# Three row normalisations of a decoder tile computed on GpSimd instead of VectorE, in tiles 0 to 13, with all engine lists written anew

## The reference, cut to what matters

```
x = layernorm(x + attn(layernorm(x)*g + b, memory))   # 8 heads, 256 memory slots, 3 retrieval steps, entmax-1.5
x = layernorm(x + xattn(x, ctx))                      # 16 heads, 64 context rows, softmax
x = layernorm(x + x @ (W * scale).T + bias)           # dense, 256 to 256
layernorm(y) = (y - mean(y)) / sqrt(var(y) + 1e-5)    # over the 256 values of a row
```

## Time and profile before

| | |
|---|---|
| median of 3 runs | 880.46 us (878.66 to 974.31) |
| the profiled execution, its own time | 881.4 us |
| its span, first to last instruction | 879.5 us |
| busy: PE, DVE, ACT, POOL | 817.2, 766.5, 736.5, 490.1 us |
| DMA | 17.63 MB, mean 20 GB/s |

### The profile page before, as it was taken

One profiled execution on the slowest core, in us unless ns is written; L12 is line 12 of the kernel. 1 busy time (PEld: TensorE's weight loads), 2 busy tenths in 40 slices (PEclk: granted clock), 3 DMA queues, 4 the chain that ended last, 5 costly groups with the idle time before them and its releaser, 6 DMA issues.

```text
span 879.5 us, 18277 instructions
## 1 busy us (share of the span) xinstructions
PE 817.2 (93%) x5598; PEld 699.7 (80%) x5598; DVE 766.5 (87%) x1915; ACT 736.5 (84%) x1781; POOL 490.1 (56%) x2304
## 2 busy tenths in 40 slices
PE   6999998899999989999988999999999998999964
PEld 5878887688898878988877888888878876887852
DVE  3699998999999999989998999999989999997451
ACT  3589997999998999979899899989989899987310
POOL 4144357465655664666754666674665757566232
PEclk9999999799999989999999999999999999999986
DMA  8900002000000000000000000000000000000000
GB/s 271 226 1 1 18 20 77 9 10 5 1 1 1 1 2 0 2 16 8 15 3 1 8 1 4 2 2 1 10 19 3 7 2 1 1 8 1 1 25 16
DMA packets 24215, 17.63 MB, mean 20 GB/s; under 512 B 11760, under 2 KB 23536, under 8 KB 23856
## 3 DMA queue, kind: packets, MB, share of 16 engines
q1 hardware_dynamic: 23872, 16.13, 6.6%
q0 software_dynamic: 240, 0.27, 0.2%
HBM read 14.30 MB, written 2.10 MB: 19 GB/s over the span
## 4 chain that ended last, share of the span: by engine, by line
PE 65%; DVE 16%; ACT 11%; POOL 4%; issue 2%; DMA 1%; SPq 0%; POOLq 0%
PE banks L1318 26%; PE banks L1341 10%; PE banks L1329 7%; PE banks L1406 6%; PE banks L1365 5%; DVE moments L859 5%; ACT work L769 4%; DVE top L839 3%; ACT work L760 2%; PE banks L1189 2%; PE banks L1376 2%; ACT work L781 2%; PE banks L1398 2%; PE banks L1419 1%; DVE work L879 1%
## 5 line engine op out<-in xcount | busy, mean ns | idle before, releaser
L859 DVE BATCH_NORM_STATS2 moments<-work 128x6 f32<-128x512 f32 x576 | 377.1, 687 | 9.4 <-ACT work L769 6.3
L1318 PE MATMUL banks<-weights_s,work 128*128 128x256 f32 x1536 | 356.4, 385 | 1.5 <-ACT work L760 0.7
L769 ACT ACTIVATE work<-work,neg_u 128x256 f32<-128x256 f32 x768 | 332.8, 524 | 22.6 <-DVE neg_u L871 17.3
L1318 PEld LDWEIGHTS banks<-weights_s,work 128*128 128x128 f32 x1536 | 288.4, 193 | 46.5 <-issue 7.7
L760 ACT ACTIVATE work<-banks,neg_low 128x256 f32<-128x256 f32 x384 | 154.5, 499 | 5.2 <-DVE neg_low L850 4.9
L839 DVE MAX8 top<-banks 128x8 f32<-128x256 f32 x384 | 141.2, 415 | 9.6 <-PE banks L1318 8.5
L1009 POOL TENSOR_TENSOR resid_sum<-moments 128x8 f32<-128x8 f32 x144 | 30.5, 212 | 210.4 <-DVE moments L859 209.1
L1329 PE MATMUL banks<-ident,work 128*128 128x128 f32 x768 | 113.1, 283 | 20.5 <-ACT work L752 8.1
L781 ACT ACTIVATE work<-banks 128x512 f32<-128x512 f32 x192 | 113.7, 613 | 15.8 <-PE banks L1329 15.6
L1329 PEld LDWEIGHTS banks<-ident,work 128*128 128x128 f32 x768 | 90.6, 145 | 37.5 <-issue 15.8
L1341 PE MATMUL banks<-weights_s,work 128*128 128x256 f32 x512 | 115.0, 380 | 0.0
(11 more groups left out here) (159 smaller groups left out, 1079.1 us busy)
## 6 DMA issues: line engine op xcount, KB each, us to landing
work<-in_L_xattn_Wo_dram SPq DMA_DIRECT2D x2, 1024.0 KB, 11.2
out_dram<-work SPq DMA_DIRECT2D x16, 128.0 KB, 1.8
work<-in_L_xattn_w_kc_q_dram SPq DMA_DIRECT2D x2, 768.0 KB, 5.8
rows<-in_L_xattn_Wq_dram SPq DMA_DIRECT2D x1, 1536.0 KB, 14.3
rows<-in_x_dram SPq DMA_DIRECT2D x1, 1536.0 KB, 6.6
work<-in_L_attn_Wq_dram SPq DMA_DIRECT2D x1, 1024.0 KB, 9.2
work<-in_L_attn_Wo_dram SPq DMA_DIRECT2D x1, 1024.0 KB, 12.1
work<-in_ctx_dram SPq DMA_DIRECT2D x32, 32.0 KB, 2.2
```

The source lines that it names most:

```text
L769: ins = nc.scalar.activation(q_resid[:, j, h, :], q_resid0[:, j, h, :], ACT.Relu, bias=small["neg_u"][:, j, h:h + 1])
L859: ins = nc.vector.bn_stats(moments[:, j, 2 * q:2 * q + 2, :].rearrange("p h k -> p (h k)"), r.rearrange("p h n -> p n h"))
L1318: ins = nc.tensor.matmul(ps_scores[:, h, :], lhsT, w[:, h, t, :], start=(t == 0), stop=(t == CT - 1))
```

## The change: what it does, and the diff

For tiles 0 to 13, `norm` is no longer a stage of DVE. Its instruction, with the same operands, follows the seventh instruction of `rstd` on POOL in the same stage, and signals `row_step` as before. That is 42 instructions (14 tiles with three each). In tiles 14 and 15 `norm` stays on DVE. The lists of turns of all five engines are new.

```diff
@@ tile_stages
-    dve, dve_tail = dve + after, dve_tail + after
+    dve_tail += after
+    dve = [what for what in dve if what[0] != "norm"] + once("residual", 1) + once("residual", 2)
@@ tile_turns (the last line of each string)
-        "PE": ...
-              "fffffbfbbcbcccccccbeebeeeceeccfefcfffffdfddcddddcdccdddeceedeeeceddeddfefeeffeffddfeefeefffefeffffff",
+        "PE": ...
+              "ffffffbbbcbcccccccebeebeececceeffcfffffdfddcdddcdccdddceedeeeeceddeddeefeffefffdfdeefeefffefeffffff",
-        "POOL": ...
-                "bdeeffcddbffdedeeecfceeffdfeecffcddbfefdedfedcefgffef",
+        "POOL": ...
+                "beedfcfbddffbdedeeecfceeffdfecefcfddeffddecfeefgeffdf",
-        "SP": "04216357109238ba4d7cfe6589dcbaef",
+        "SP": "20156374a20983176bed54fc8ab9dcef",
...
@@ POOL, stage rstd, behind the seventh instruction
+                        if in_tail(p, j):
+                            return
+                        pool.wait_ge(rstd_step[j], step(RSTD_OPS))
+                        if s == 2 and p:
+                            pool.wait_ge(out_stored[j], p * 16)
+                        nc.gpsimd.tensor_scalar((q_out if s == 2 else q_row)[:, j, :], q_y[:, j, :], row_mv[:, j, 0:1],
+                                                row_rstd[:, at], ALU.subtract, ALU.mult).then_inc(row_step[j], 1)
```

More of the change, by code:

```diff
@@ new lines, in tile_turns @@
+        "DVE": "hhhhhh0hhh0h00100h000021h00110011001h1020h1202102h20h0h21h102h02h02h11211h211h011110201h1002122h0020"
+               "202h020221h021212h11h0001h11010h210120312h1011h22h101222213h21213023033h1203h13331223h3103230323h023"
+               "20322h303323hh3hh23113111000403603012033300035303031030300337033010323212322131331223221121202341434"
+               "21441212114a418440141433232344344030434334134344595454425522202333345234325445450535434443354b535452"
+               "45445643636546465556656d65546116360476767677c6464166566754761566557755575766575474657657655715675674"
+               "555456475775464226564144466762464752675655546444764477646774465266477775547574e435537777565757656635"
+               "6534778725578888575773888f86886566885858448676387667776648864868569968696989684999977797986979796988"
+               "97988599899888596878a77aa5aa579479aa8aa888aa978aa89aa998a8a8858988aaaa797a798a979a769897688858988989"
+               "9789869bb6b8bb8889b98989bb9aabaa9ab896b8a8a8aba8b897abab79b89b99aaba9a999babb8a97ca9cbaacbbcca6cb9a7"
+               "ccac9a99ccbb9c9bcbcc79c9cb99bba9ab9c9ababcaccaabbabcbca988aab8bdaaacadddad7babbbdd8cbcdbbdcccaddaaac"
+               "cccda8cacdaddcbcdcdcbdcbcbdbddcbacbcbce9d9dcedcbceeeb9b98bebebbdedbedbdeed9bbbdbdcdbebbdaadedeeccddc"
+               "eddecaadbdeeececf9fcdefcdffddecaceffffccffefadfffbdfefedeecfcfffbdfecdfdcfdedeecccebcefbfefeffceecff"
+               "fefdecdddbfefeeefffefdedcefdddfdbfdfdffdedfedfefeedcceedeeddcefeffeffeceefffefedeefeefceeeffffdfdfdd"
+               "cfefeffdfffeeeeeedefefeeffffffegfffffefg",
@@ new lines, in tile_turns @@
+        "ACT": "hhhhhhhh01h0000h0000211101h00h0h22h2h2h0h1h01h11002h0111102h22110h1100h022h2210102h02h102h2111h02010"
+               "h1211h0h3222211112h202h03h3033020h33h3302222h333h310111021031022333131311000043363352000033332072003"
+               "0303321202211132233223011141040443131841411443031323442443232494445550343045010022242342344335255544"
+               "434553133536566264103546616456554155776666a73b741666655556167715751754544664675554576772215544454656"
+               "5625627744447675567252675642424477677366636746477475445557334265767336575635387777884874888347855555"
+               "6685646748787864476646488c988999856899996766556989989868775798889854daaa9ae95777569aa9aa858858aaaa88"
+               "788969698589a7aa7a77798898879966898898a6b9b9b6a78b8668f98aa99a97bab798b9b8aaa8a88b99b989bb7aa6a9abbb"
+               "bc79cc7bcb899aa7ac7c7cc9ab999bbabca9c9c9c9a9babab9b8a88c8aaaab7bccbcdbdcdacda9bab8bb8ca8c8ccdddbdaca"
+               "bacccaaddaddcbcc9cbb89b9dd9cdcdcaceebbedbb99de99bdbbebdddeacabcbbeebdbddbadaeecce9eacabdcdadadfefefe"
+               "fbcecabfefffcedcdfdfdeffeedebdffbcffcdcdcdfdefeeebbfffbfbcccecceefefcffeedebdeddffcffddedecfdcfffeee"
+               "efdfcdddedeecfeffdfcceecceefdfffdedceeeeddfedddfdffeffefffefedeeffefffff",
@@ new lines, in tile_turns @@
+        "POOL": "hh000010101022211112200022010111122200131332233232h3hhh000010033300332111323221011414422343433440120"
+                "2335550443435524455660630664164671757557575155466614747466224416654777455527755334227753888656683683"
+                "7646485869649977799898986754574aaa88aa885aa7979958588989766889b9bb688aaabb99a9ab98b76a6a7ccc99cc9b9b"
+                "bac7acbaab9a7a7bb88dddaccac8ddccbdacdcbb8b998bebee9bbdddecedadab9e9eccdcafffadffacffceeecbbdceeffddf"
+                "beedfcfbddffbdedeeecfceeffdfecefcfddeffddecfeefgeffdf",
```

7 lines of the change are left out of this document (added).

## The result

The changed kernel took 889.86 us (median of 4 runs, 889.23 to 890.60), beside 880.84 us for the kernel before. One of the four runs of before, 974.31 us, fell in a slower state of the chip and is left out of the ratio, which is 1.011, with a 95% interval of 1.0089 to 1.0131. The change is slower by 9.0 us on these medians, by 9.4 beside the 880.46 us that the other three runs of before have as their median. Its time lies 2.9 us above the top of my range. The forecast, a gain of 5 us, had the wrong sign. The execution that the profile shows took 890.03 us, with a span of 888.1 us; the one of before had 881.4 and 879.5.

What follows compares the result with a forecast made beforehand. PE was taken as the bound, DVE and ACT nearly level where PE stalls. Gains of 5 (relief) and 2 (sooner rows) less 2 (Newton steps) took 881.4 to 876.4, by the runs' median 875.5, called 875 us; range 863 to 887.

Steps and rivals of the forecast that it cites:

- relief and port: DVE's work: 18.7 us relieved less 2.7 us held at the memory port, of which a third, 5 us, was credited.
- sooner rows: Normed rows start a step after their roots on POOL; PE's one wait of 2.2 us credited as 2 us gained.
- Newton steps: Newton arithmetic queued behind the normed row on POOL comes later, at most 23 us summed; charged a tenth, 2 us.
- lists 0: New order of turns on all engines: not priced, bounded by PE's idle 22.5 us either way, taken as nothing.
- DVE loses 42 instructions: Normed rows leaving DVE: 42 by 0.404 us is 17.0 us, with 1.7 us idle before them 18.7 us.
- PE is the bound: Rival: PE busy for 96% of 190 to 800 us, so nothing moves, 878 to 884 us; chance 0.22.
- I take 0.55 us: Length of one normed row on POOL, between a fill's 0.34 us and the two-tensor biased row's 729 ns.
- That load is hidden by POOL's idle time: POOL's added 23 us (14 to 31) was held covered, since POOL waited 139 us on `moments` alone.
- The port, 2.7 us: DVE instructions held at the port shared with POOL: 42 x 0.23 x 0.28 us; bounds nothing and 23 us.
- third rival: Slower by the lock: POOL's normed row delays Newton arithmetic and holds DVE's clip or weights, 887 to 900 us; chance 0.16.
- The end from 840 keeps its length: Sign for the forecast: the last stretch, tile 15's serial chain, stays as long, as its normed row stays on DVE.
- ACT's wait for `neg_u`: Sign that the lock decides: this wait, with longer means of L874, L871 and L879, grows well over 13 us.

Runs made afterwards that it cites:

- e12_none_old: Kernel before with its old lists, 42 normed rows struck from DVE, a 0.19 us POOL instruction in each row's place, normalisation of tiles 0 to 13 left out: 879.51 us.
- e12_none_new: Changed kernel, new lists with mended end, a 0.19 us POOL instruction in place of each normed row, normalisation of tiles 0 to 13 left out: 883.60 us.
- e6_whole_end: Changed kernel with list ends mended: DVE's flag before the last normed row, POOL's third roots of tiles 14 and 13 and tile 13's row moved: 885.86 us.
- e4_old_lists: Changed kernel, rows on POOL, but with the lists of the kernel before, the moved rows only struck from DVE's: 895.41 us, ratio 1.0183.
- e13_both: Kernel before, rows kept on DVE, and the same 42 rows also made on POOL into a buffer nobody reads: 902.52 us, ratio 1.0239.

## Why the prediction was wrong

The sum that the runs give, by medians, from 880.84: relief of DVE, net of 0.19 us a row on POOL, -1.3 (e12_none_old); new lists' body +4.1 (e12_none_new against e12_none_old, 883.60 - 879.51); the rows on POOL in those lists +2.3 (e6_whole_end against e12_none_new); the end of the lists +4.0 (the change against e6_whole_end). By the ratios the four are -1.2, +4.0, +3.5 and +3.4. Each term is a step from one kernel to the next, so they must add up to the whole, and that they do is no check. The medians come from different chips, so each term has about 2 us of doubt.

Beside my own terms (relief and port -5, sooner rows -2, Newton steps +2, lists 0) this says where the 14 us between the forecast and the result lie: 8.1 in the lists that I took at nothing, 3.7 in the relief, 2 in the sooner rows, and almost none in the rows' cost on POOL (2.3 where I had charged 2). That last number is close by luck. The new lists had made the row cheap, at a price of their own; in the order that I knew, the same rows cost 17 us, and the whole change 16 instead of a gain of 5. With the rows on POOL the lists as a whole save 6.4 us (16.1 to 9.7 by the ratios), so neither half of the change stands alone.

Step by step, as I put them:

- **"DVE loses 42 instructions", 17 us off its work: right in kind, less in amount.** The groups' busy times fell by 14.4 us: 17.3 less in the rows, 2.9 more elsewhere, most of it in the held lines below. What reached the end was mis-sized. I took "a third, 5 us"; it was 1.3. I had read that PE carries 65% of the chain. But that kernel doesn't prove the rival "PE is the bound" either: 4.2 us more stood ready near the end and were lost behind `worst_all`, a stand of POOL that my sum doesn't have. Whether a third is wrong without it stays open.
- **"I take 0.55 us": failed.** 1.24 us measured, outside both bounds. I took the two-tensor instruction for the dearest form because it reads most. The nearest row by shape was not the nearest by form: no instruction on POOL of before was a two-operation one with values a partition, so the upper end had no row behind it.
- **"That load is hidden by POOL's idle time", charged with "a tenth, 2 us": failed; in the old order it is the step that turned the sign.** In the lists that I knew, the row costs 16 + 1.2 = 17 us beside the kernel with 0.19 us in its place, which is 0.4 us for each of the 44 us added. Even at about my 0.55 us it is not a tenth: at 0.40 it costs 2.3 us, at 0.61 6.7, so around 5 us where I charged 2. The wait of 139 us for `moments` is POOL idle while nothing is due; what counts is the moments in which it is not. The row of one tile runs then in front of another tile's Newton step. I named that very queue, and who waits for it, and then priced it by an average.
- **"The normed row comes sooner", +2 us: not seen.** No kernel has this part alone. In e12_none_old the readers may go as soon as the root is there, and that and all of DVE's relief together are 1.3 us net.
- **The port, 2.7 us: the holding is there, the price is not shown.** The means of the four DVE lines after (L872, L875, L880, L848) are 202, 228, 373 and 261 ns, where they were 169, 219, 367 and 255. That is (33 + 9 + 6) x 48 ns and 6 x 192 ns, 3.5 us. It looks like my 2.7, but the rows are not its cause in the main: in e12_none_new, which has the new lists and no row, the four lines are already 2.2 us above before, so the rows add 1.3. In the old lists they add nothing (+1.7 in e12_none_old, +1.5 in e4_old_lists, which lost 16 us). And my formula with the measured length gives 42 x 0.52 x 0.62 = 13 us, ten times what the rows add; the nearness of 2.7 to 3.5 is luck. Two of the lines, after:

```profile
L872 DVE SCALAR_TENSOR_TENSOR neg_u<-delta,neg_limit x48: 116/156/758, 38.1 to 796.5; 128x8 f32<-128x8 f32 x48
L875 DVE TENSOR_TENSOR neg_u<-neg_u_raw,neg_limit x48: 115/168/992, 46.0 to 808.9; 128x8 f32<-128x8 f32 x48
```

  The trace holds single instructions (116 ns at the shortest, 758 at the longest), so it agrees with the lock rule of the Trainium skill, "SBUF — State Buffer", section Who interferes with whom, in kind; the 3.5 us, and DVE's unchanged 766.7 us in e13_both, say that it is not what made the kernel slower. My third rival was right in its sign and its time, and had two causes, "the lock" and the Newton steps behind; only the second holds, and for the old lists. In the changed kernel most of the loss is the order's.
- **The rule of one-input work at line rate:** the Trainium skill, "GPSIMD Engine Reference", section Engine selection, sets GpSimd beside VectorE: about twice as slow for two-input work, roughly line-rate for one-input. By the rows, the product of two tensors on POOL takes 0.72 us, and DVE's two-tensor sum of the same shape (one of them from PSUM) 0.42, so 1.7 times as slow, which agrees in the main. The normed row, with one tensor, takes 1.23 us on POOL and 0.404 on DVE, three times as long, which doesn't agree. The measurement decides.
- **"The new lists ... take nothing": failed, and it is the largest part of the miss in the changed kernel.** They make the row cheap, 2.3 us (3.5 by the ratios) instead of 17, but for that the order of the whole body costs 4.1 us and the last tile 4.0. My bound of 22.5 us on either side holds the net of both; the middle of a bound is not a price. "The end from 840 keeps its length" was wrong for the same reason. I had the new lists before me in the diff, and the place of `g`, the flag, against the last `f` stands in the last line of DVE's.
- **"What would show it":** ACT's wait for `neg_u` was to tell the slower rival, "well over 13 us". From 190 to 800 it is 13.9 after, so by that sign it would have been denied. The lists had made that wait short again, and the time went into PE's other waits; e4_old_lists, with 28.5 beside 17.3 over the span, shows it as the sign predicted.

What stays open: why the new lists' body costs 4 us by itself, and which engine's list does it; no kernel here has one engine's old list with the others' new ones. Open too is what the relief of DVE brings without POOL's stand behind `worst_all`.

## What to carry to other kernels

An engine with 44% of idle time is not a place where work is free. Ask what stands behind the new instruction in that engine's queue and how long the chain through it is; an idle share, or a long wait of that engine for others, says nothing about the moment at which the instruction lands. Price an instruction by its own form: take a tensor and two values a partition for a form of its own, and when the trace has none, put a few of them behind the kernel's work and read their lengths before the move. And where a move comes with a new order of all the work, read the last tile's order item by item, since there every swap lies on the path, while the middle of the order is priced only by running it without the moved work. A kernel with the work left out shows a net value: look in its chain for what took back the time that it had won.

## What the runs showed of the hardware

- A `tensor_scalar` on POOL (128x256 f32) takes 1.23 us with two operations by values of a partition and 0.93 with one, while a product of two tensors takes 0.72 and the subtraction of a broadcast value, as a two-tensor form, 0.61. Half the width of the first takes 0.80, so 3.4 ns an element and 0.37 us on top.
- Around `worst_all` POOL stands for 5.7 us before the instruction and 7.16 us after it ("issue": it waits for nothing that the profile shows), while the instruction takes 0.38 us. In e6_whole_end the gap after it is 7.15 us, ended by a DVE result, and before it 5.61:

```profile
864.15 0.38 POOL L1152 PARTITION_ALL_REDUCE worst_all<-worst  x1 [5.61 <-issue]
871.68 0.18 POOL L1056 TENSOR_TENSOR row_var<-row_mv,eps_col 128x1 f32<-128x1 f32 x1 [7.15 <-DVE row_mv L935]
```

  In the kernel before the root stood 6.65 us behind it, released by DVE's `row_mv`, so part of such a gap may be waiting for DVE. In two kernels it was POOL's own: in e4_old_lists the sum that the root reads ended 3.6 us before the root started (gap 7.11 us), in e12_none_old 4.2 us before it (gap 7.5 us). There the stand is on the path.
